# An attention loop over 392 groups of 16 nodes: scores two groups ahead of the weighted sum, row transposes in three pieces between the products, eight slots of gathered rows

## The reference

```python
q, k, v = x @ Wq.T + bq, x @ Wk.T + bk, x @ Wv.T + bv      # 8 heads of 32
e       = edge_attr @ We.T                                  # one row of 256 for each edge
alpha   = sum(q[dst] * (k[src] + e), -1) / sqrt(32)         # a score for each edge and head
ex      = exp(alpha - segment_max(alpha, dst)[dst])
out     = segment_sum((v[src] + e) * ex / segment_sum(ex, dst)[dst], dst)
# then: skip connection, layernorm, gelu layer, layernorm, experts with a top-2 gate
```

## Time and profile before

| | |
|---|---|
| median of 3 runs | 4067.2 us (4065.84 to 4069.83) |
| profiled execution: its time / its span | 4068.84 / 4067.0 us |
| PE busy | 91% of the span |
| POOL, DVE, ACT busy | 50%, 48%, 41% |
| mean granted TensorE clock | 0.952 |
| weighted sums of the second stage | 392, from 238.82 us to 2991.51 us |

### The profile page before, as it was taken

How to read it: one execution, slowest core, us unless ns; L and a number is a source line. 1 busy time by engine, 2 the same in 40 slices (tenths; PEclk the granted TensorE clock), 3 DMA queues, 4 the chain that set the end, 5 groups by cost and what they waited for, 6 DMA issues and landing times. The chain is left out here.

```text
span 4067.0 us, 77637 instructions
## 1 busy us (share of the span) xinstructions
PE 3700.7 (91%) x22914; PEld 2352.3 (58%) x22914; DVE 1970.6 (48%) x5552; ACT 1681.0 (41%) x3636; POOL 2046.7 (50%) x2100
## 2 busy tenths in 40 slices
PE   5879999999999999999999999999967888888888
PEld 2346666666666666666666666666645555555555
DVE  5344444444444444444444444444446555555544
ACT  2134444444444444444444444444424343433442
POOL 3067777777777777777777777777720000000000
PEclk9989999999999999999999999999988888888887
DMA  6467677776777767777776777767740000000000
GB/s 200 156 164 186 181 184 184 189 186 183 185 185 186 187 184 187 186 185 189 187 190 183 185 188 186 182 183 190 188 105 21 15 26 16 21 16 22 13 13 13
DMA packets 637776, 572.41 MB, mean 141 GB/s; under 512 B 430486, under 2 KB 523991, under 8 KB 637700
## 3 DMA queue, kind: packets, MB, share of 16 engines
q0 software_dynamic: 159616, 429.57, 35.9%
q1 hardware_dynamic: 478100, 142.10, 16.8%
HBM read 632.99 MB, written 33.05 MB: 164 GB/s over the span
## 5 line engine op out<-in xcount | busy, mean ns | idle before, releaser
L610 POOL DMA_INDIRECT F<-kv_rows,srcg x1970 | 1994.7, 1013 | 841.2 <-issue 564.4
L688 DVE COPY PT<-pPT 128x384 f32<-128x384 f32 x393 | 219.0, 557 | 1164.9 <-PE pPT L878 1146.4
L885 PE MATMUL pZ<-F,PT 128*64 128x320 f32 x4704 | 743.1, 434 | 0.0
L858 PE MATMUL ring<-ident,F 128*128 128x128 f32 x3940 | 605.8, 285 | 120.6 <-ACT FT L790 111.9
L858 PEld LDWEIGHTS ring<-ident,F 128*128 128x128 f32 x3940 | 420.3, 141 | 406.4 <-ACT FT L790 203.9
L796 ACT ACTIVATE Pw<-pS,nMn 128x384 f32<-128x384 f32 x393 | 226.8, 577 | 954.5 <-DVE nMn L683 954.5
L790 ACT ACTIVATE FT<-ring 128x512 f32<-128x512 f32 (+1 forms) x1182 | 579.1, 525 | 73.4 <-PE ring L858 10.4
L1170 POOL DMA_DIRECT2D out_dram<-accb x13 | 9.7, 749 | 1047.1 <-DVEq L1332 1047.1
L885 PEld LDWEIGHTS pZ<-F,PT 128*64 128x64 f32 x4704 | 366.4, 136 | 254.5 <-issue 0.5
L867 PE MATMUL pS<-FT,qh 128*64 128x320 f32 x3144 | 512.0, 447 | 1.5 <-issue 1.1
L682 DVE TENSOR_REDUCE nmx<-pS 128x1 f32<-128x384 f32 x393 | 219.2, 558 | 202.1 <-PE pS L871 200.5
(11 more groups left out here) (215 smaller groups left out, 4458.0 us busy)
## 6 DMA issues: line engine op xcount, KB each, us to landing
F<-in_edge_attrT SPq DMA_DIRECT2D x788, 80.0 KB
F<-kv_rows,srcg POOLq DMA_INDIRECT x1970
F<-in_dst SPq DMA_DIRECT2D x788, 20.0 KB
srci<-src_front SPq DMA_DIRECT2D x796, 1.5 KB, 3.5
kv_rows<-kvs SPq DMA_DIRECT2D x7, 1792.0 KB, 6.7
qb<-q_cols SPq DMA_DIRECT2D x100, 64.0 KB, 2.9
U<-in_x SPq DMA_DIRECT2D x7, 896.0 KB, 10.9
xn_rows<-xs SPq DMA_DIRECT2D x7, 896.0 KB, 6.7
```

The lines of the kernel that those rows point to most:

```text
L610: pool.indirect_dma_start(out=F[s][:, t, 0:KV], out_offset=None, in_=kv_d, in_offset=bass.IndirectOffsetOnAxis(ap=srcg[j % GB][:, col:col ...
L688: dve.tensor_copy(PT[:, :, :], pPT[:, 0:SW].rearrange("p (t r) -> p t r", r=P)).then_inc(pt_emptied, 1)
L858: m = pe.transpose(ring[n % 2][:, k * w + (t - t0) * P:k * w + (t - t0 + 1) * P], F[j][:, t, k * P:(k + 1) * P], ident[:, :])
L885: m = pe.matmul(pZ[rows, 0:ZW], PT[:, t, rows], F[s][:, o * TO + t, D:FP], start=(t == 0), stop=(t == KB - 1))
```

## The change

Step j now has PE's work in this order: scores of group j+2; four transposes of group j+3; zt of group j-1; two transposes of group j+3; g3 or project where due; weighted sum of group j; ea_rows of j+1; pt of j+1; four transposes of group j+4. ACT follows in the same order. `Pw` has two buffers. `F` has eight slots, and the gather of group j+6 waits for the weighted sum of group j-2. SP loads the edges of group j+4 and the indices of group j+8 after ea_rows of group j (`ea_filled`), where it waited for `slot_free`. DVE does `neq` for group j+3 behind `maximum` of group j+2. g3 moves from steps 2 and 5 to steps 0 and 4. Ahead of the loop there is more work: six groups are gathered, not two; 34 transposes and two sets of scores are done, not 20 and one; POOL clears the four new slots.

```diff
-                F = [sbt(s2, f"F{i}", [P, T, FP]) for i in range(SLOTS)]
+                F = [sbt(s2, f"F{i}", [P, T, FP]) for i in range(GB)]
-                Pw = sbt(s2, "Pw", [P, SW])
+                Pw = [sbt(s2, f"Pw{i}", [P, SW]) for i in range(2)]
-                IDX, F3N, AHEAD = 32, 64, 6
+                IDX, F3N, AHEAD, GA = 32, 64, 8, 6
...
-                                    sp.wait_ge(slot_free, it * GB + (j + 3))
+                                    sp.wait_ge(ea_filled, it * GB + (j + 1))
                                     sp.sem_inc(load_turns, 1)
-                                    load_edges(at[k], at[k + 1], j + 2)
+                                    load_edges(at[k], at[k + 1], j + SLOTS)
...
-                        pool.wait_ge(blank, 12)
-                        for j in range(2):
+                        for s in range(SLOTS, GB):
+                            pool.memset(F[s][:, :, 0:KV], 0.0).then_inc(blank, 1)
+                        pool.wait_ge(blank, 17)
+                        for j in range(GA):
...
-                                    pool.wait_ge(slot_free, it * GB + (j + 3))
+                                    pool.wait_ge(slot_free, it * GB + (j + GA + 1))
-                                    gather(j + 2)
+                                    gather(j + GA)
...
-                                    neq((j + 2) % SLOTS, bass.ds(b * GB + (j + 2), 1), it * (2 * F3N) + F3N * ((j + 2) // SLOTS + 1))
...
-                                    maximum((j + 1) % GB, it * GB + (j + 2))
+                                    maximum((j + 2) % GB, it * GB + (j + 3))
+                                    neq((j + 3) % SLOTS, bass.ds(b * GB + (j + 3), 1), it * (2 * F3N) + F3N * ((j + 3) // SLOTS + 1))
...
-                                    weights((j + 1) % GB, it * GB + (j + 2))
-                                    act.wait_ge(slot_free, it * GB + (SLOTS + j + 1))
+                                    m = j * len(PAIRS)
+                                    weights((j + 2) % GB, it * GB + (j + 3))
+                                    ft_out(j + 3, 1, RING0 + m, rb + (m + 1))
+                                    ft_out(j + 3, 2, RING0 + m + 1, rb + (m + 2))
...
+                                    act.wait_ge(slot_free, it * GB + (GB + j + 1))
                                     act.activation(Zs[:, :], pZ[:, 0:ZW], ACT.Copy).then_inc(z_out, 1)
-                                    for q in range(len(PAIRS)):
-                                        m = j * len(PAIRS) + q
-                                        ft_out(j, q, RING0 + m, rb + (m + 1))
-                                    ea_out((j + 1) % SLOTS, it * GB + (j + 2))
+                                    ea_out((j + 1) % GB, it * GB + (j + 2))
+                                    ft_out(j + 4, 0, RING0 + m + 2, rb + (m + 3))
...
+                                    scores((j + 2) % GB, (j + 2) % SLOTS)
+
+                                    pe.wait_ge(ring_emptied, rb + (m - 1))
+                                    ft(s3, 1, RING0 + m)
...
+                                    pe.wait_ge(z_out, it * GB + (j + 1))
+                                    zt((j + GB - 1) % GB)
+
                                     pe.wait_ge(ring_emptied, rb + m)
...
+                                    ft(s3, 2, RING0 + m + 1)
...
                                     pe.wait_ge(pt_emptied, it * GB + (j + 1))
-                                    pe.wait_ge(z_out, it * GB + (j + 1))
                                     for t in range(KB):
-                                        z = z_part(s, t)
+                                        z = z_part(j, t)
                                     z.then_inc(slot_free, 1)
...
                                     ea_rows((j + 1) % SLOTS)
 
                                     pe.wait_ge(p_done, it * GB + (j + 2))
-                                    pt()
...
+                                    pt(j + 1)
+
+                                    pe.wait_ge(gathered[s4], it * (16 * T) + 16 * T * ((j + 4) // GB + 1))
+                                    pe.wait_ge(ring_emptied, rb + (m + 1))
+                                    ft(s4, 0, RING0 + m + 2)
```

More of the change, by code:

```diff
@@ L514, in build @@
                 f3_landed = [sem(f"f3_landed{i}") for i in range(SLOTS)]
-                gathered = [sem(f"gathered{i}") for i in range(SLOTS)]
-                IDX, F3N, AHEAD = 32, 64, 6
+                gathered = [sem(f"gathered{i}") for i in range(GB)]
+                IDX, F3N, AHEAD, GA = 32, 64, 8, 6
                 slot_free, idx_ready = sem("slot_free"), sem("idx_ready")
@@ L575, in _ @@
                         sp.dma_start(We[:, :, :], a["W3"].rearrange("(k p) f -> p k f", p=P)[:, :, 0:DE]).then_inc(we_landed, 16)
-                        for j in range(2):
+                        for j in range(SLOTS):
                             load_edges(at[2 * j], at[2 * j + 1], j)
@@ L601, in _ @@
                             sp.sem_inc(load_turns, 1)
+                            sp.wait_ge(f3_landed[SLOTS - 1], done * (2 * F3N) + F3N)
+                            sp.sem_inc(load_turns, 1)
                     @block.gpsimd
@@ L625, in _ @@
                                 for j in range(GB):
[L627 removed]
+                                    pool.wait_ge(slot_free, it * GB + (j + GA + 1))
                                     pool.sem_inc(gather_turns, 1)
[L630 removed]
+                                    pool.wait_ge(idx_ready, it * GB + (j + GA + 1))
                                     pool.sem_inc(gather_turns, 1)
[L632 removed]
+                                    gather(j + GA)
+                        it = blocks_done(pool, longest)
+                        for j in range(SLOTS, GA):
+                            pool.wait_ge(gathered[j], it * (16 * T) + 16 * T)
+                            pool.sem_inc(gather_turns, 1)
                     @block.vector
@@ L636, in _ @@
                         ch = Chain(dve, "dve2")
-                        dve.sem_inc(slot_free, SLOTS)
+                        dve.sem_inc(slot_free, GB)
                         for o in range(2):
@@ L728, in _ @@
                         ch.step(dve.tensor_copy(nMo[:, :], nM[:, 0, :]))
-                        for j in range(2):
+                        for j in range(3):
                             neq(j, slice(j, j + 1), F3N)
@@ L732, in _ @@
                         pt_out(1)
+                        maximum(1, 2)
                         base = ch.n
@@ L818, in _ @@
                                 n += 1
-                        weights(0, 1)
-                        ea_out(0, 1)
+                            if j == 1:
+                                weights(0, 1)
+                                ea_out(0, 1)
+                        weights(1, 2)
+                        ft_out(3, 0, n, n + 1)
                         longest, loop = long_loop(act)
@@ L874, in scores, with pt @@
                             m.then_inc(s_done, 1)
-                        def pt():
+                        def pt(j):
                             for t in range(KB):
-                                m = pe.transpose(pPT[:, t * P:(t + 1) * P], Pw[:, t * P:(t + 1) * P], ident[:, :])
+                                m = pe.transpose(pPT[:, t * P:(t + 1) * P], Pw[j % 2][:, t * P:(t + 1) * P], ident[:, :])
                             m.then_inc(pt_filled, 1)
@@ L927, in _ @@
                                 n += 1
-                        pe.wait_ge(ring_emptied, n)
+                        pe.wait_ge(ring_emptied, len(PAIRS))
                         pe.wait_ge(neq_done, 1)
                         pe.wait_ge(g3_emptied, 1)
-                        pe.wait_ge(blank, 12)
+                        pe.wait_ge(blank, 17)
                         scores(0, 0)
                         ea_rows(0)
-                        pe.wait_ge(p_done, 1)
-                        pt()
+                        pe.wait_ge(gathered[2], 16 * T)
+                        for q in range(len(PAIRS)):
+                            pe.wait_ge(ring_emptied, n - 1)
+                            ft(2, q, n)
+                            n += 1
+                        pe.wait_ge(p_done, 1)
+                        pt(0)
+                        pe.wait_ge(neq_done, 2)
+                        scores(1, 1)
+                        pe.wait_ge(gathered[3], 16 * T)
+                        pe.wait_ge(ring_emptied, n - 1)
+                        ft(3, 0, n)
                         longest, loop = long_loop(pe)
```

69 lines of the change are left out of this document (32 added, 37 removed).

## The result

| | before | changed |
|---|---|---|
| time, median of 3 runs (us) | 4067.2 | 3917.9 (3916.5 to 3917.9) |
| ratio to before, 95% interval | | 0.963 [0.961, 0.965] |
| span of the profiled execution (us) | 4067.0 | 3914.8 |
| one block | 56.32 | 53.10 |

The kernel is 149 us faster. This is what the first comparison gives; on the chips of the experiments, further down, it is not so. The windows view of the new second stage answers to the earlier trace rows: the columns are the same.

The account below looks back on a forecast made before the run. PE was taken as the bound: first weighted sum at 245, plus 49 blocks of 53.1, less 7.1, gives 2840, 151 less; 1 us less behind it gives 3917 profiled, 3915 median. Range for 8 in 10: 3878 to 3990.

Parts of the forecast that it names:

- The ordinary step: PE's usual step in a block: 5.46 us of work plus five array-size switches of 0.15, 6.21 instead of 6.54.
- the new kind: Switch from column halves to row halves, weighted sum to pM, not in the earlier trace: taken as 0.15 us.
- The ring wait: PE's row transposes waiting for ACT to empty a `ring` bank: 0.48 us a step, all to be gained.
- the wait moves on: Rival, chance 0.10: ACT's chunk behind `weights`, or merge and G3 copy before pM, takes back half the 0.48: 4013 us.
- pZe as a piece of 64 columns: Rival, chance 0.14: going from pZe back to row transposes is a sixth switch, 59 us more: 3974 us.
- g3, project, the block: PE's additions to a block's steps: g3 0.86 us each, twice, project 1.69; block 53.1 against 56.3.
- The start: First weighted sum, after the longer work ahead of the loop: at 244 to 245 us, taken as 245, against 238.82.
- The last weighted sum: End of PE's weighted sums in the second stage: forecast at 2840 us, where it was 2991.5.
- The interval behind the last weighted sum: Piece subtracted at the end of the 49 blocks: 7.1 us, from 6.21 + 0.86.
- Late indices: Rival, chance 0.09: index transfers landing over 3.2 us late hold DVE's `join_indices`, then PE every step; slower, 4260 us.
- POOL: Gathers of 1.30 us each, 52.0 a block, 1.1 below PE's block; POOL waits about 1.1 a block for weighted sums.
- In steady state the deeper gathers buy nothing: PE showed no wait for gathered rows before; gathering further ahead is needed only because PE reads rows two groups earlier.

## Why the prediction was right, and where not

The prediction was 3915 us, the measurement 3917.9. It held by its steps, not by luck of a sum. The 3 us between them are mostly the spread of runs: the profiled execution was forecast at 3917 and took 3916.5, but lay 1.4 under the median, where that of before had lain 1.6 over it.

- **The ordinary step**, 5.46 of work and five switches of 0.15: 6.21 forecast and measured. With one switch more 6.36, with three 5.91: the price of 0.15 is confirmed both ways, and with the new kind (column halves to row halves, weighted sum to pM) among the five the sum comes out at the same price.
- **The ring wait** goes, all 0.48 of it. The page shows 10.4 us of idle before row transposes in the whole kernel, all of it for gathered rows and none for ACT, and 1.0 before scores:

```profile
L872 PE MATMUL ring<-ident,F 128*128 128x128 f32 x3954 | 649.9, 279 | 10.4 <-DMA F<-kv_rows,srcg 10.4
```

  The rival "the wait moves on" is what the simpler edit (two transposes behind Pw's) ran into; the changed order did not.
- **pZe as a piece of 64 columns**: no. pZe to transposes takes 0.11, the time of one transpose. The Trainium skill, "TensorEngine Tiling (Array Packing)", section Restrictions and Gotchas, excludes FP32 transposes from column tiling; the trace agrees with it here.
- **g3, project, the block**: 1.69 for project and 0.86 for each g3, by the intervals (8.27 - 6.21 - 0.37 and 0.49 + 0.37): as forecast, 53.10 against 53.1.
- **The start**: 244.21, forecast 244 to 245. The last weighted sum: 2839.4, forecast 2840. The tail behind it was 1075.5 and is 1075.4, where I had taken 1 us off. The interval behind the last weighted sum is 6.70, where 7.1 was taken. These are misses of 0.8, 0.9 and 0.4 us that partly cancel; no more than that was luck.
- **Late indices**: `srci` holds DVE for 1.5 us in all between 500 and 2800 us, 4 times.
- **POOL**: a small miss. I had it wait 1.1 a block for weighted sums; by the waits of 500 to 2800 us it waits 0.5 for them and 1.2 for DVE's indices, and its gathers take 1.28, not 1.30; so PE's block stood 2.0 above POOL's, not 1.1:

```profile
POOL F L612 <- DVE srcg L675: 52.2, 133, 0.9
POOL F L612 <- PE pZ L899: 21.0, 69, 0.3
DVE srcg L671 <- DMA srci<-src_front: 1.5, 4, 0.9
```

- **"In steady state the deeper gathers buy nothing"**: where the prediction was tested the block is PE's sum and nothing more, which fits it, though depth alone was not run there; and with one gather in five the gain is there without the depth. On the experiments' chips it missed a cost: there depth alone costs 12%, and the changed kernel loses 6%. No rival of mine had this; the slower one (late indices) was another mechanism, and the trace of before could not show it, since in it even runs of up to 20 gathers delay no signal of TensorE (0.014 to 0.024 us).

## What to carry to other kernels

When one engine is in flight nearly all the time, price its list from the starts of its pieces, and count the places where it changes the array's size: here that gave a 4% change to within 0.1%. A chunk moved out of the way of a full buffer needs a consumer that is far enough away; else the wait only moves. Before deeper prefetch is added to a kernel that doesn't wait for data, measure on more than one chip: the kernel with it kept to PE's sum in the first comparison, and depth alone cost 12% on another chip. Here the whole change gave 4% in one place and lost 6% in the other.

## What the runs showed of the hardware

- A change between full-size, 64-row and 64-column work costs PE 0.15 us at the full clock (undisturbed steps of 5.91, 6.21 and 6.36 us with three, five and six of them), in two parts: 0.09 to 0.10 at the change and 0.05 to 0.06 at the next start. An FP32 transpose with a 64-column left side among full-size ones costs none (0.11 to the next start).
- On a chip of the experiments, while GpSimd issued indirect DMAs one behind another, TensorE's signals came 0.9 to 5.2 us late on the mean (up to 10.7) from the 2nd gather of a run on, its short instructions had unexplained gaps of over 1 us, and its granted clock was 0.89 instead of 1.00. Another of these chips shows the late signals too. With a fifth of the gathers the two kernels' signals came 0.017 and 0.018 us late and the granted clock was 1.00. Why the kernel before takes 4067 us in the first comparison and about 4750 on all five chips of the experiments is open: that it is the chip, and not something else that differed between the two, isn't shown. Whether gathers set apart in time would avoid the delay at full number wasn't tried.
